# A new order for all engines and a new first load in a four-layer linear-attention stack on one core

## The reference, cut to what matters

```python
for i in range(4):                      # x: 2 batches x 2048 tokens x 128
    q, k, v = x @ Wq[i] + bq[i], x @ Wk[i] + bk[i], x @ Wv[i] + bv[i]
    Q, K = elu(q) + 1, elu(k) + 1
    KV, Ksum = sum_s(K * v), sum_s(K)   # per channel, over the whole sequence
    V = Q * KV / (Q * Ksum + 1e-6)
    a = gelu(gelu(V @ Wo[i] + bo[i]))
    x = ln(a + x, ln1_s[i], ln1_b[i])
    x = ln(gelu(gelu(x @ W1[i] + b1[i]) @ W2[i] + b2[i]) + x, ln2_s[i], ln2_b[i])
x = layernorm(input + x)
h = gelu(x @ absmean(W_fc).T)           # weights of -1, 0, 1
x = layernorm(x + (layernorm(h) * ln_w + ln_b) @ absmean(W_proj).T)
```

## Time and profile before

| | us |
|---|---|
| median of 3 runs | 502.14 (500.6 to 503.85) |
| the profiled execution | 501.86 |
| its span, first to last instruction | 500.1 |
| PE busy | 449.2 (90%) |
| DVE busy | 406.9 (81%) |
| ACT busy | 398.1 (80%) |
| POOL busy | 21.0 (4%) |

### The profile page before, as it was taken

One profiled execution on the slowest core, in us unless ns is written; L12 is line 12 of the kernel. 1 busy time (PEld: TensorE's weight loads), 2 busy tenths in 40 slices (PEclk: granted clock), 3 DMA queues, 4 the chain that ended last, 5 costly groups with the idle time before them and its releaser, 6 DMA issues.

```text
span 500.1 us, 6588 instructions
## 1 busy us (share of the span) xinstructions
PE 449.2 (90%) x2074; PEld 310.8 (62%) x2074; DVE 406.9 (81%) x1378; ACT 398.1 (80%) x554; POOL 21.0 (4%) x23
## 2 busy tenths in 40 slices
PE   7587998999899989998999899989999979989990
PEld 6455565656565656466646665666557547879890
DVE  5887879877996898689978986997689997956586
ACT  2877898979888988889898989898996657739271
POOL 2400000000000000000000000000002040100000
PEclk9988999999999999999999999999999998989995
DMA  8100000000010000001000000000002101001012
GB/s 279 59 2 0 0 23 1 1 0 1 2 41 2 22 0 1 1 1 42 1 1 0 1 0 2 0 1 1 0 10 76 32 11 43 1 1 43 2 49 78
DMA packets 5217, 10.40 MB, mean 21 GB/s; under 512 B 832, under 2 KB 1856, under 8 KB 5184
## 3 DMA queue, kind: packets, MB, share of 16 engines
q1 hardware_dynamic: 5184, 9.99, 5.9%
HBM read 7.90 MB, written 2.10 MB: 20 GB/s over the span
## 4 chain that ended last, share of the span: by engine, by line
PE 65%; DVE 21%; ACT 10%; issue 3%; DMA 1%; SPq 0%; ACTq 0%; DVEq 0%
PE tile L1112 17%; PE tile L1090 9%; PE tile L1086 9%; PE tile L1131 8%; PE tile L1087 8%; PE tile L1125 5%; PE tile L1202 5%; PE tile L1191 2%; DVE xl L702 2%; DVE nt L680 2%; ACT aa L365 2%; ACT nt L380 2%; ACT x L394 2%; DVE x L690 1%; DVE stats L673 1%
## 5 line engine op out<-in xcount | busy, mean ns | idle before, releaser
L1112 PE MATMUL tile<-h,w 128*128 128x512 f32 x256 | 113.2, 593 | 0.1
L1086 PE MATMUL tile<-xh,wh 128*128 128x512 f32 x224 | 96.5, 431 | 14.0 <-DVE xh L696 4.3
L1087 PE MATMUL tile<-xh,wl 128*128 128x512 f32 x224 | 88.7, 396 | 0.0
L1112 PEld LDWEIGHTS tile<-h,w 128*128 128x128 f32 x256 | 47.6, 190 | 53.3 <-issue 52.4
L372 ACT ACTIVATE h<-tile,vec 128x1024 f32<-128x1024 f32 x64 | 69.2, 1117 | 9.8 <-PE tile L1090 9.4
L380 ACT ACTIVATE nt<-tile,work 128x128 f32<-128x128 f32 x176 | 65.0, 467 | 15.1 <-DVE work L667 15.1
L1090 PE MATMUL tile<-xl,wh 128*128 128x512 f32 x224 | 72.3, 404 | 0.4
L1086 PEld LDWEIGHTS tile<-xh,wh 128*128 128x128 f32 x224 | 42.0, 188 | 37.1 <-issue 10.7
L673 DVE BATCH_NORM_STATS2 stats<-tile 128x6 f32<-128x128 f32 x256 | 53.5, 280 | 1.9 <-PE tile L1131 1.9
L1131 PE MATMUL tile<-ident,nt 128*128 128x128 f32 x288 | 40.7, 284 | 11.7 <-DVE nt L680 9.9
L1090 PEld LDWEIGHTS tile<-xl,wh 128*128 128x128 f32 x224 | 41.3, 189 | 14.3 <-DVE xl L702 4.2
(11 more groups left out here) (176 smaller groups left out, 698.2 us busy)
## 6 DMA issues: line engine op xcount, KB each, us to landing
x<-x_t SPq DMA_DIRECT2D x8, 512.0 KB, 5.3
out_r<-x SPq DMA_DIRECT2D x8, 256.0 KB, 2.1
raw_u<-layers SPq DMA_DIRECT2D x4, 256.0 KB, 2.7
w<-layers SPq DMA_DIRECT2D x4, 256.0 KB, 3.0
raw_a<-layers SPq DMA_DIRECT2D x4, 192.0 KB, 2.4
wo<-layers SPq DMA_DIRECT2D x4, 64.0 KB, 4.1
fc<-fc_t SPq DMA_DIRECT2D x1, 256.0 KB, 5.8
proj<-proj_t SPq DMA_DIRECT2D x1, 256.0 KB, 5.7
```

What stands on the lines that cost most here:

```text
L1086: pe.matmul(dst, wh[:, w0:w0 + P], xh[:, part(n, p, at)], start=True, stop=False)
L1087: pe.matmul(dst, wl[:, w0:w0 + P], xh[:, part(n, p, at)], start=False, stop=False)
L1112: mm = pe.matmul(dst, w2[:, (t - 1) // 2 % 2, j * P:(j + 1) * P], h[:, p, j * PAIR + at:j * PAIR + at + BANK], start=(j == 0), stop=(j == ...
```

## The change

Every stream but SP's middle is put in another order, and all tables of PSUM tiles are new (a table of its own for step 1; step 2 is now written out, the loop runs over steps 3 to 6). What the order moves, with the diff at the places used later:

- The first pair of `x` is loaded by ACT in two halves; its exp tables are loaded ahead of the first use, DVE makes the high part half by half, and the first product may begin with the first half.
- The high parts of pairs 2 and 3 move from POOL to ACT, their low parts from POOL to DVE. `shifted` of pair 0 moves from POOL to DVE, `with_constant` of pair 3 from DVE to POOL.
- `moments` can now take several norms; every call gives it one. In a step the chains of norm 2 and of norm 1 (both p=1) stand one behind the other.
- ACT loads its tables 19 times instead of 24. DVE writes 116 instead of 80 rows of norms 1 and 2 (L680), ACT 140 instead of 176 (L380).

```diff
@@ the first loads @@
             sp.dma_start(vec[:, :, :], vectors_in).then_inc(vec_in, 16)
-            load_x(0)
+
             load_x(1)
...
+            act.dma_start(x[:, 0:BANK], x_in[:, 0:BANK]).then_inc(half_loaded, 16)
+            act.dma_start(x[:, BANK:PAIR], x_in[:, BANK:PAIR]).then_inc(x_loaded[0], 16)
+            exp_tables()
             act.wait_ge(vec_in, 16)
             act.wait_ge(b_ready, 2)
             key_neg(0, 0)
-            exp_tables()
             key_exp(0, 0)
+            query_neg(0, 1)
+            query_exp(0, 1)
+            first_high_of(2)
@@ high part of pair 0, on DVE @@
+                eng.wait_ge(half_loaded, 16)
+                eng.tensor_copy(xh[:, 0:BANK], x[:, 0:BANK]).then_inc(b_ready, 1)
+                eng.wait_ge(x_loaded[p], 16)
+                eng.tensor_copy(xh[:, BANK:PAIR], x[:, BANK:PAIR]).then_inc(x_hi["2"][q], 1)
@@ ACT, the loop @@
                 gelu_once(t, 1)
                 gelu_twice(t, 1)
+                gelu_up(t - 1, 0, 0)
                 gelu_once(t, 0)
+                gelu_up(t - 1, 0, 1)
                 gelu_twice(t, 0)
-                gelu_up(t - 1, 0, 0)
-                gelu_up(t - 1, 0, 1)
                 gelu_up(t - 1, 0, 2)
                 gelu_up(t - 1, 0, 3)
+                rows("1", t, 1, 1)
+                rows("1", t, 1, 0)
                 rows("2", t, 1, 0)
                 rows("2", t, 1, 1)
-                rows("1", t, 1, 1)
-                rows("1", t, 1, 0)
                 gelu_down(t, 0)
                 whole("1", t, 1)
-                rows("1", t, 0, 0)
+                whole("2", t, 1)
                 high("2", t, 1)
-                whole("2", t, 1)
                 whole("1", t, 0)
@@ DVE, the loop @@
                 row_stats("2", t, 1)
+                row_stats("1", t, 1)
                 first_sum(t, 0)
-                moments("2", t, 1)
-                row_stats("1", t, 1)
-                moments("1", t, 1)
+                moments(("2", t, 1))
+                moments(("1", t, 1))
                 row_stats("1", t, 0)
-                moments("1", t, 0)
+                if t % 2 == 0:
+                    take_up(t // 2)
+                moments(("1", t, 0))
                 rows("1", t, 0, 1)
+                rows("1", t, 0, 0)
                 second_sum(t, 0)
                 high("1", t, 1)
-                if t % 2 == 0:
-                    take_up(t // 2)
                 low("1", t, 1)
@@ PE, the loop @@
                 down(t, 1, 1, False)
+                up(t - 1, 0, 0)
+                fold_out(t)
                 attention_out(t, 1)
-                fold_out(t)
                 attention_out(t, 0)
-                up(t - 1, 0, 0)
                 turned("2", t, 1)
                 up(t - 1, 0, 1)
+                turned("1", t, 1)
                 up(t - 1, 0, 2)
                 up(t - 1, 0, 3)
-                turned("1", t, 1)
                 turned("1", t, 0)
...
-                back("1", t, 0, 1)
-                back("2", t, 1, 0)
                 back("1", t, 0, 0)
                 turned("2", t, 0)
+                back("1", t, 0, 1)
@@ POOL @@
-            first_high(pool, 2)
-            first_low(pool, 2)
-            first_high(pool, 3)
-            first_low(pool, 3)
             shifted(pool, 1)
-            shifted(pool, 0)
+            with_constant(pool, 1)
             shifted(pool, 2)
+            shifted(pool, 3)
             with_constant(pool, 0)
-            with_constant(pool, 1)
-            shifted(pool, 3)
             with_constant(pool, 2)
+            with_constant(pool, 3)
```

More of the change, by code:

```diff
@@ L479, in _ @@
             gelu_up(0, 0, 3)
-            rows("2", 1, 1, 0)
+            rows("1", 1, 0, 0)
+            rows("1", 1, 0, 1)
             rows("2", 1, 1, 1)
-            rows("1", 1, 1, 1)
-            rows("1", 1, 1, 0)
             gelu_down(1, 0)
             whole("1", 1, 1)
-            rows("1", 1, 0, 0)
-            high("2", 1, 1)
+            whole("1", 1, 0)
+            high("1", 1, 0)
             whole("2", 1, 1)
-            whole("1", 1, 0)
             gelu_up(1, 1, 0)
             gelu_up(1, 1, 1)
+            rows("2", 1, 0, 0)
             gelu_up(1, 1, 2)
-            rows("2", 1, 0, 1)
             gelu_up(1, 1, 3)
-            for t in range(2, STEPS - 1):
+            key_neg(2, 1)
+            exp_tables()
+            key_exp(2, 1)
+            key_neg(2, 0)
+            key_exp(2, 0)
+            query_neg(2, 0)
+            query_exp(2, 0)
+            query_neg(2, 1)
+            query_exp(2, 1)
+            share_log(2, 0)
+            share(2, 0)
+            share_log(2, 1)
+            share(2, 1)
+            gelu_down(2, 1)
+            gelu_once(2, 1)
+            gelu_twice(2, 1)
+            gelu_up(1, 0, 0)
+            gelu_once(2, 0)
+            gelu_up(1, 0, 1)
+            gelu_twice(2, 0)
+            gelu_up(1, 0, 2)
+            gelu_up(1, 0, 3)
+            rows("1", 2, 1, 1)
+            rows("1", 2, 1, 0)
+            rows("2", 2, 1, 0)
+            rows("2", 2, 1, 1)
+            gelu_down(2, 0)
+            whole("1", 2, 1)
+            whole("2", 2, 1)
+            high("2", 2, 1)
+            whole("1", 2, 0)
+            gelu_up(2, 1, 0)
+            gelu_up(2, 1, 1)
+            gelu_up(2, 1, 2)
+            rows("2", 2, 0, 0)
+            gelu_up(2, 1, 3)
+            for t in range(3, STEPS - 1):
                 key_neg(t, 1)
@@ L922, in _ @@
-            constant_part(1)
+            query_round(1, 0)
+            first_sum(0, 0)
+            queries(1, 0)
+            fold_kv(1)
+            row_stats("1", 0, 0)
+            moments(("1", 0, 0))
+            rows("1", 0, 0, 1)
+            constant_part(1)
+            take_attention(1)
+            rows("1", 0, 0, 0)
+            whole("1", 0, 0, False)
+            high("1", 0, 0)
+            first_sum(1, 0)
+            low("1", 0, 0)
+            centered_projection()
             second_sum(1, 1)
@@ L933, in _ @@
+            rows("1", 1, 1, 1)
+            rows("2", 1, 1, 0)
             second_sum(1, 0)
@@ L943, in _ @@
             low("2", 1, 0)
-            for t in range(2, STEPS - 1):
+            low("1", 1, 0)
+            keys(2, 1)
+            values(2, 1)
+            keys(2, 0)
+            values(2, 0)
+            fold_kv(2)
+            query_round(2, 0)
+            queries(2, 0)
+            query_round(2, 1)
+            queries(2, 1)
+            constant_part(2)
+            second_sum(2, 1)
+            first_sum(2, 1)
+            row_stats("2", 2, 1)
+            row_stats("1", 2, 1)
+            first_sum(2, 0)
+            moments(("2", 2, 1))
+            moments(("1", 2, 1))
+            row_stats("1", 2, 0)
+            take_up(1)
+            moments(("1", 2, 0))
+            rows("1", 2, 0, 1)
+            rows("1", 2, 0, 0)
+            second_sum(2, 0)
+            high("1", 2, 1)
+            low("1", 2, 1)
+            row_stats("2", 2, 0)
+            moments(("2", 2, 0))
+            low("2", 2, 1)
+            rows("2", 2, 0, 1)
+            high("1", 2, 0)
+            whole("2", 2, 0, False)
+            high("2", 2, 0)
+            low("2", 2, 0)
+            for t in range(3, STEPS - 1):
                 keys(t, 1)
@@ L999, in _ @@
+            rows("1", 7, 0, 1)
             rows("1", 7, 0, 0)
-            moments("2", 7, 1)
+            rows("2", 7, 1, 1)
+            low("1", 7, 1)
             second_sum(7, 0)
-            high("1", 7, 0)
+            outer_sum(1)
             low("1", 7, 0)
             row_stats("2", 7, 0)
-            moments("2", 7, 0)
+            moments(("2", 7, 0))
+            shifted(dve, 0)
             rows("2", 7, 0, 0)
-            first_sum(7, 1)
-            outer_sum(1)
+            row_stats("x", 0, 1)
```

628 lines of the change are left out of this document (343 added, 285 removed), and 29 rows, old and new, of tables (LAST_SLOTS, SECOND_SLOTS, SLOTS, TAIL_SLOTS).

## The result

The changed kernel takes 524.09 us (median of 4 runs, 523.32 to 524.33) against 502.22 us (median of 4, 500.6 to 503.85): a ratio of 1.042 with a 95% interval of 1.039 to 1.046. It is slower by 22 us. The direction was forecast, the size was not: 513 was predicted, with a range up to 521. The profiled execution took 524.24 us, with a span of 522.4.

The account below looks back on a forecast made before the run. PE was taken to set the pace, with about 2.5 us idle a step and a nearly slackless chain of waits. 501.86 - 4 (beginning) + 8.7 (loop) + 5.5 (tail) + 1 (clock) = 513.1, range 498 to 521.

Parts of the forecast that it names:

- The beginning, -4: Start of the kernel: half loads and early tables put ACT 4.1 us earlier, carried through to step 2; -4 us.
- `key_neg` "behind the first product's six matmuls": Beginning: with the table load moved ahead, ACT's first `key_neg` starts at 7.7 and `key_exp` at 8.8.
- The loop, +8.7: Loop and written-out step 2: three even steps at +2.1 and two odd at +1.2 make +8.7 us.
- the term for the clock: Behind the tail's PE stall of 7.6 us: granted clock may fall once more; +1 us, of 0 to 3.
- The loss is on ACT: Loop: ACT waits 3.7 us instead of 1.15 for norm 1's rows, so gelu of `down` starts 2.7 us later.
- the high end of the range: Loop: +12 us if DVE's four extra rows (1.1 us) are also exposed in every even step.
- `take_up`'s 1.1 us: Even loop steps: `take_up` now stands ahead of p=0's chain, 1.1 us with little hidden; an even step costs +2.1.
- The tail, +5.5: Last step: later `second_sum` delays pair 1's second load, so DVE and PE wait for `outer_sum`; +5.5 us, of +3 to +8.
- counting `with_constant` calls: Tail: by the skill's contention rule, four on POOL instead of three would cost one more DVE stall, 2.2 us.
- B: Rival for the loop: PE's idle 2.5 us a step and moved products cover the later gelu; 504.4 us, chance 0.22.
- C: Rival for the loop: ACT's load sets the step, so moving rows off it shortens steps; 493.7 us, chance 0.16.
- D: Rival for the tail: clock stays low 8 us behind the stall and DVE meets POOL twice; about 519 us, chance 0.14.

Follow-up runs that it names:

- the split of rows: Changed kernel with ACT writing norm 2's rows first, plus half of norm 1's p=0 rows back from DVE to ACT in steps 2 to 6: 513.67 us against 522.9.
- the pair: Changed kernel with the p=1 chains of norm 2 and norm 1 interleaved instead of in succession in steps 2 to 7: 504.67 us.

## Why the prediction was right or wrong

**The beginning, -4: wrong, it was -1.8.** The step that failed is `key_neg` "behind the first product's six matmuls" at 7.7. The product needs the low part too, which DVE makes only after both halves of the high one, so ACT began at 8.98 and `key_exp` at 10.13: 2.8 us earlier than before instead of 4.1. One more of it went on the way, where PE waits 2.13 us at 21.80 and 3.58 at 40.09, each followed by windows of 4 us at a clock from 0.52 to 0.82. Before there was a pause of 1.89 at 22.80 with a window at 0.62, and 2.54 at 41.52. That a lead of ACT at the start is carried through to step 2 was assumed, and wasn't worked out.

**The loop, +8.7: too small, it was +15.3, for a reason I had not seen and by a path I had half seen.** The waits were replayed well. ACT's wait was forecast at 3.7 us and measured at 3.67. A step without the fall of the clock is 49.15 (odd) and 50.3 (even), where 49.5 and 50.4 had been given. The step that failed is the term for the clock: it had been priced for the tail's long stall alone ("A stall of 7.6 us may bring this once more") and at nothing in the loop, although rows 8 showed that a pause of PE in the middle of dense work lowers it. It costs 1.6 us in each of five steps, 8.1 us, of the 11 by which 513 fell short of 524. The path by itself is 15.3 - 8.1 = 7.2 us, less than the 8.7 forecast. The whole sum, as measured: 501.9 - 1.8 + 7.2 + 8.1 + 8.8 = 524.2.

The sentence "The loss is on ACT" was wrong as a cause. DVE's path was late by as much: the four rows that were moved to it stood in the chain and had been put at nothing but the high end of the range. Undoing ACT's order (522.9) or exchanging the chains (524.12) won about nothing; giving DVE less to do ahead of p=0 won 9 (the split of rows) and 19 us (the pair), path and clock together. That the forecast of the path came out near its measure, by ACT alone, was luck in part: undoing what it priced won nothing.

`take_up`'s 1.1 us was nearly right as a delay ahead of p=0's rows: `second_sum` starts 0.8 us later behind `whole` in an even step than in an odd one. As the cost of its new place it was too much, since behind `second_sum` it had been on the path too: 0.25 us a step, and the 7 us that its return won are nearly all clock.

**The tail, +5.5 and +1 for the clock: +8.8.** Its mechanism stood, its sizes were off both ways. `second_sum` was forecast 6 us later and is 5.7 later than the loop left it; the waits were put at 8.0 (DVE) and 7.6 (PE) and are 6.78 and 6.52; PE's second `up` waits for the outer sum as the order said. The stall with its clock cost 8.9, of which 8.9 - 6.5 = 2.4 is clock (0.50 and 0.84 over 8 us) instead of 1. What was undervalued on the other side is the rest of the new tail: without the stall it is 120.8 us from that sum to the end, against 126.6 before. More than half of that is the meeting of DVE and POOL. Before, three operations of norm chains took 2.34, 2.27 and 2.14 us instead of 0.17, each beside POOL; after, one does, beside `with_constant`, and one takes 0.98 beside `shifted`, although POOL has four `with_constant` instead of three:

```profile
438.36 0.98 DVE L744 SCALAR_TENSOR_TENSOR work<-work 128x8 f32<-128x8 f32 x1
439.30 2.40 POOL L304 TENSOR_TENSOR nt<-nt,cb 128x1024 f32<-128x1024 f32 x1
439.38 2.35 DVE L747 SCALAR_TENSOR_TENSOR work<-work 128x8 f32<-128x8 f32 x1
```

All of these DVE operations stand in the chain that ended last. They cost 6.2 us before and 3.0 after, so 3.2 of the 5.8 us; where the rest comes from isn't shown. What the Trainium skill ("SBUF — State Buffer", section "Who interferes with whom") says of two-input DVE instructions holds for the two that met POOL; counting `with_constant` calls, as the prediction did, said nothing of how many would meet.

**The rivals.** B (the loop absorbs the lateness) and C (ACT's load sets the step) are out: the steps are 3 us longer, with ACT's load smaller. D (the clock stays low behind the stall, 519) named the right agent in the wrong place. The range ended at 521, since the bound of the clock term was taken from one stall and not from one in each step.

What stays open: why the clock stays at 1.00 in the kernel before with one order exchanged, where PE was busy for 1.53 of 4 us, and falls in the changed kernel behind 2.21 of 4. No experiment here separates the length of a pause from what PE did before it, and the executions of one program at 524.5 and 518.3 us say that the program alone doesn't settle it.

## What to carry to other kernels

Look first at which engines hold the chain that ended last, and not at busy shares, which hardly changed here. When a change makes PE pause in every step, cost the pause twice, once for its length and once for the clock that may fall behind it, and look at the clock's column of the windows for whether the present kernel is close to that. Follow every engine's path up to the place where they meet: undoing the late one first seen wins nothing when another is late by the same amount. Two chains of small dependent operations, given to an engine alternately, cost little more than one.

## What the runs showed of the hardware that was not expected

- The same instructions with the same waits (0.74, 0.33 and 0.71 us) ran at a granted clock of 1.00 in one kernel and of 0.85 and 0.72 in another, and a step of 49.2 us became one of 50.8.
- Two chains of fourteen DVE operations on 128x8, nearly all waiting for the one before, took 2.75 us when interleaved and 4.75 in succession.
- Executions of one program differed by 6 us, 518.3 at a mean granted clock of 0.969 and 524.5 at 0.953.
- A PE stall of 6.5 us cost 8.3 to 8.9 us of the time.
